# Grouping the transposed softmax probabilities by query tile in an attention block, with tile 3 taken first

## The chip, the cores and the metric

The kernel runs on one core of a Trainium2 chip. The metric is the device time of one execution in microseconds; the kernel before took 309.45 us (median of 3 runs, 309.11 to 309.55). Below, PE is the matmul engine, ACT the scalar engine, DVE the vector engine, POOL the GpSimd engine, SP the engine that issues the DMAs.

## The reference, cut to what matters

For two sequences of 512 rows of width 256: attention with 16 heads that share one key, which is also the value; then a residual sum and layer norm; then a feed-forward net on the half of the rows that a router picks; then another sum and layer norm. The change touches only the attention:

```
k = x @ W_lat + b_lat                      # 512 x 128, key and value of all heads
q = x @ W_d + b_d                          # per head 512 x 128
att = softmax(where(causal, q k^T / sqrt(128), -inf))
y = att @ k
out = concat(y) @ W_proj + b_proj
```

## The kernel before

**Units and periods.** A unit is one head of one sequence: 32 units. The code runs in periods, software-pipelined by hand: in period p the engines work on unit p (scores, softmax), unit p+1 (query projection), unit p-1 (transposing the probabilities, product with the values) and unit p-2 (output projection). Periods 3 to 12 are a hardware loop, the others are written out. Periods 18 to 27 also hold, in small pieces, the layer norm and the router of sequence 0: one "early piece" and one "late piece" a period on DVE (`early_piece` L944, `late_piece` L966). In periods 13 to 28 POOL also splits a part of the feed-forward weights.

**Precision.** Most products are made of three fp32r matmuls, hi*hi, hi*lo, lo*hi (`product`, L355). So each operand that comes out of PSUM is split: ACT copies the rounded high part, DVE subtracts it from the PSUM bank to get the low part.

**Tiles.** 512 queries are four tiles j of 128, 512 keys four tiles i. Because of the mask, query tile j has scores only for keys of tiles 0 to j. For each j, DVE adds the mask, takes the negated maximum and writes the scaled scores to SBUF (`maxima`, L885), ACT takes the exponential and the row sums (`exps`, L710), DVE takes the reciprocal of the sums (L936), and the tiles are scaled: tile 3 on ACT (L755), tiles 2, 1, 0 on DVE (L941), at the end of the period. In the next period PE transposes the ten 128x128 blocks P(j,i) in three turns (`turn`, L441), each turn into one PSUM bank, and ACT and DVE split what each turn has left in the bank (`turned`, L717 and L895).

**Before, a turn is a key tile.** Turn 0 is the four blocks of key tile 0, bank `ps_t0`; turn 1 the three of key tile 1, bank `ps_t1`; turn 2 the blocks (3,3), (2,2), (3,2), again in `ps_t0`. Block (3,3) is kept in plain fp32 (`pT_last`). Each key tile lies in one run of columns of `pT_hi` and `pT_lo`, and `values` (L493) makes one product for each key tile: 512, 384 and 256 columns wide, then the fp32 block.

**Order of one period.** PE: scores of tiles 3 and 2, turns 0 and 1, scores of 1 and 0, queries of the next unit (six matmuls of 512 columns), turn 2, output projection (twelve of 256), values. ACT: high part of y; turned 0 and 1; exponentials of 3 and 2; query high part; turned 2; exponentials of 1 and 0; scaling of tile 3. DVE: low part of y (`yT_lo`); maxima of 3; early piece; turned 0; maxima of 2; turned 1; maxima of 1 and 0; query low part; turned 2; reciprocal; late piece; scaling of 2, 1, 0. POOL: once all three scalings are done, it splits the next weights (four instructions, six in periods 13 to 28).

Turn 2 writes the bank that turn 0 used, so PE waits at L448 for DVE's turned 0. Turn 0 waits for all scalings (L446, L447). The last periods differ: period 31 makes no queries, and there turn 2 comes after the output projection, so the values follow turn 2 at once; period 32 is the same with gather matmuls in place of the scores.

Of the kernel before, what the change touches and what calls it, by code (L numbers as in the profile page):

```python
# [34 lines left out]
P = 128  # L35
# [17 lines left out]
PT_OFF = {2: 0, 1: 2 * P, 0: 5 * P}  # L53
PT_COLS = 9 * P


def mk_layer_kernel(nc, x, W_lat, b_lat, W_d, b_d, W_proj, b_proj, router_w, router_b,
                    w1, b1, w2, b2, out):
    with ExitStack() as top:
# [30 lines left out]
        negmax = sb("negmax", [P, 2, TILES])  # L90
        sums = sb("sums", [P, 2, TILES])
# [122 lines left out]
        def p_tile(s, j):  # L214
# [139 lines left out]
        def _(pe):  # L354
# [86 lines left out]
            def turn(at, n):  # L441

                p, s = at.p, at.place(-1)
                tiles, dst, _, _ = turns[n]
                if n == 0:
                    wait(pe, norm_act, p)  # L446
                    wait(pe, norm_dve, p * 3)  # L447
                wait(pe, pt_lo_done, p * 3 - (3, 4, 2)[n])  # L448
                if n == 1 and at.fixed - 1 in (AT_TURN, AT_SELECT, AT_RANK):

                    pe.wait_ge({AT_TURN: score_row_done, AT_SELECT: rank_row_done, AT_RANK: rank_done}[at.fixed - 1][0], 1)
                if at.fixed == 1 and n < CH:
                    pe.wait_ge(x_split, CH + n + 1)
                a = 0
                for i in tiles:
                    for j in range(i, TILES):
                        last = pe.transpose(dst[:, a:a + P], p_tile(s, j)[:, i * P:(i + 1) * P], ident[:, :])  # L457
                        a += P
                last.then_inc(pt_ready, 1)
# [33 lines left out]
            def values(at):  # L493

                p, b = at.p, at.batch(-1)
                if at.fixed - 1 == b * HEADS:
                    pe.wait_ge(k_split, b + 1)
                    pe.wait_ge(k_last_done, b + 1)
                wait(pe, y_lo_done, p - 1)
                for i in range(TILES - 1):  # L500
                    wait(pe, pt_lo_done, p * 3 - 2 + i)
                    n = (TILES - i) * P
                    t = slice(PT_OFF[i], PT_OFF[i] + n)
                    product(ps_y[:, SEQ - n:], (k_hi[b][:, i, :], k_lo[b][:, i, :]),
                            (pT_hi[:, t], pT_lo[:, t]), i == 0, False)
                wait(pe, pt_last_done, p)
                pe.matmul(ps_y[:, SEQ - P:], k_last[b][:, :], pT_last[:, :], start=False, stop=True).then_inc(y_ready, 1)  # L507
# [168 lines left out]
        def _(act):  # L676
# [40 lines left out]
            def turned(at, n):  # L717
                wait(act, pt_ready, at.p * 3 - 2 + n)
                if n == 2:
                    act.copy(pT_last[:, :], ps_t0[:, 0:P]).then_inc(pt_last_done, 1)  # L720
                act.copy(pT_hi[:, turns[n][3]], turns[n][2]).then_inc(pt_hi_done, 1)  # L721

            def period(at):
# [118 lines left out]
        def _(dve):  # L842
# [52 lines left out]
            def turned(at, n):  # L895
                wait(dve, pt_hi_done, at.p * 3 - 2 + n)
                _, _, src, dst = turns[n]
                dve.tensor_tensor(pT_lo[:, dst], src, pT_hi[:, dst].bitcast(F32), ALU.subtract).then_inc(pt_lo_done, 1)  # L898

            def period(at):  # L900
                p = at.p
                if at.live(0):
                    wait(dve, scores_ready, p * 3 + 1)
                if at.live(-2):
                    wait(dve, y_hi_done, p - 1)
                    dve.tensor_tensor(yT_lo[:, :], ps_y[:, :], yT_hi[:, :].bitcast(F32),  # L906
                                      ALU.subtract).then_inc(y_lo_done, 1)
                if at.live(0):
                    maxima(at, (3,))
                early_piece(at)  # L910
                if at.live(0):
                    wait(dve, scores_ready, p * 3 + 2)
                if at.live(-1):
                    turned(at, 0)
                if at.live(0):
                    maxima(at, (2,))
# [7 lines left out]
                if at.fixed == 0:  # L924
                    x_low(1, 1)
                    k_low(0)
                if at.live(1) and at.fixed >= 0:
# [3 lines left out]
                if at.live(-1):  # L931
                    turned(at, 2)
                s = at.place(0)
                if at.live(0):
                    wait(dve, exp_done, p * 4 + 4)
                    dve.reciprocal(rinv[:, s, :], sums[:, s, :]).then_inc(rinv_done, 1)  # L936
                late_piece(at)
                if at.live(0):
                    wait(dve, rinv_done, p + 1)
                    for j in (2, 1, 0):  # L940
                        dve.tensor_scalar(p_tile(s, j), p_tile(s, j), rinv[:, s, j:j + 1], None,  # L941
                                          ALU.mult).then_inc(norm_dve, 1)
# [350 lines left out]
```

## Time and profile before

| | |
|---|---|
| median of 3 runs | 309.45 us |
| the profiled execution's own time | 309.75 us |
| its span | 307.9 us |
| PE busy | 290.8 us (94%) |
| DVE busy | 229.6 us (75%) |
| ACT busy | 211.8 us (69%) |
| POOL busy | 147.0 us (48%) |
| matmul instructions | 1962 |

The span is the stretch in which instructions ran; the execution's own time is 1.85 us longer. Matmuls overlap in the pipeline, so a matmul's record is longer than the distance to the next one's start: the pace of PE is read from starts. Below, a period is measured from one start of the fp32 value matmul (L507) to the next.

### The profile page before, as it was taken

How to read it: one execution, taken by the hardware profiler on the slowest of the kernel's cores; microseconds unless marked ns; L12 is line 12 of the kernel's file. 1: busy time of each engine (PE TensorE's matmuls, PEld its weight loads, DVE VectorE, ACT ScalarE, POOL GpSimd, SP SyncE). 2: the span in 40 equal slices, each digit the busy share in tenths (PEclk: the TensorE clock that was granted, in tenths of full speed). 3: DMA queues.
4: the chain of work that ended last, by engine and by line, in shares of the span. 5: the costliest groups of instructions: out<-in, count | busy, mean ns of one | idle time of the engine just before them, and what ended most of it. 6: DMA issues, size and time to landing. Idle time of an engine off the chain costs nothing.

```text
span 307.9 us, 6338 instructions
## 1 busy us (share of the span) xinstructions
PE 290.8 (94%) x1962; PEld 262.5 (85%) x1962; DVE 229.6 (75%) x698; ACT 211.8 (69%) x585; POOL 147.0 (48%) x202
## 2 busy tenths in 40 slices
PE   7999999999999999999999998999999999985991
PEld 4878999999999999999998797788999999875990
DVE  2678777777777777778888878977887775886574
ACT  3688777777777777777776785686877777541632
POOL 3557433333333485555575564577583111672021
PEclk9999999999999999999999999999999999998998
DMA  6591111111111111111111111111100000000013
GB/s 192 103 326 48 35 36 34 34 34 34 34 34 34 34 35 36 34 38 34 34 36 34 35 36 35 35 26 44 27 19 27 21 0 0 3 0 2 0 35 104
DMA packets 17739, 13.44 MB, mean 44 GB/s; under 512 B 1433, under 2 KB 17458, under 8 KB 17714
## 3 DMA queue, kind: packets, MB, share of 16 engines
q1 hardware_dynamic: 17714, 13.13, 14.8%
q8 instruction: 13, 0.21, 0.3%
q14 instruction: 12, 0.10, 0.1%
HBM read 12.07 MB, written 1.05 MB: 43 GB/s over the span
## 4 chain that ended last, share of the span: by engine, by line
PE 78%; DVE 12%; ACT 4%; issue 2%; SPq 1%; DMA 1%; POOLq 0%; DVEq 0%; ACTq 0%
PE bank L358 15%; PE bank L360 14%; PE bank L359 14%; PE bank L457 10%; PE ps_out L358 5%; PE ps_out L359 5%; PE ps_out L360 5%; PE bank L507 2%; PE bank L437 2%; DVE ties L1055 1%; DVE sel L1034 1%; DVE probs L891 1%; DVE beats L1050 1%; DVE pT_lo L898 1%; PE bank L545 1%
## 5 line engine op out<-in xcount | busy, mean ns | idle before, releaser
L714 ACT ACTIVATE probs<-probs,negmax 128x512 f32<-128x512 f32 (+3 forms) x128 | 72.6, 575 | 13.1 <-DVE negmax L891 11.8
L1158 POOL TENSOR_TENSOR wd_hi<-wd_raw,zero 128x256 fp32r<-128x256 f32 x32 | 23.8, 743 | 95.0 <-DVE probs L941 89.0
L721 ACT CAST pT_hi<-bank 128x512 fp32r<-128x512 f32 (+2 forms) x96 | 43.5, 488 | 32.7 <-PE bank L457 32.7
L891 DVE CUSTOM_DVE_ANT_0 probs<-bank,mask_row 128x512 f32<-128x512 f32 (+3 forms) x128 | 59.1, 481 | 0.6 <-PE bank L360 0.6
L898 DVE TENSOR_TENSOR pT_lo<-bank,pT_hi 128x512 fp32r<-128x512 f32 (+2 forms) x96 | 52.8, 551 | 7.3 <-ACT pT_hi L721 7.2
L457 PE MATMUL bank<-ident,probs 128*128 128x128 f32 x320 | 45.7, 273 | 2.1 <-DVE pT_lo L898 2.1
L457 PEld LDWEIGHTS bank<-ident,probs 128*128 128x128 f32 x320 | 37.9, 140 | 9.7 <-DVE pT_lo L898 4.2
L358 PE MATMUL ps_out<-wp_hi,yT_hi 128*128 128x256 f32 x128 | 38.7, 302 | 0.1
L358 PE MATMUL bank<-kT_hi,qT_hi 128*128 128x512 f32 (+2 forms) x96 | 37.6, 392 | 0.2 <-DVE qT_lo L845 0.2
L906 DVE TENSOR_TENSOR yT_lo<-bank,yT_hi 128x512 fp32r<-128x512 f32 x32 | 22.1, 690 | 20.1 <-PE bank L360 14.0
L360 PE MATMUL ps_out<-wp_hi,yT_lo 128*128 128x256 f32 x128 | 36.1, 282 | 0.0
L359 PE MATMUL ps_out<-wp_lo,yT_hi 128*128 128x256 f32 x128 | 36.1, 282 | 0.0
L358 PE MATMUL bank<-pT_hi,k_hi 128*128 128x512 f32 (+2 forms) x96 | 32.9, 343 | 0.6 <-DVE pT_lo L898 0.6
L360 PE MATMUL bank<-kT_hi,qT_lo 128*128 128x512 f32 (+2 forms) x96 | 32.5, 339 | 0.0
L359 PE MATMUL bank<-pT_lo,k_hi 128*128 128x512 f32 (+2 forms) x96 | 32.4, 337 | 0.0
L359 PE MATMUL bank<-kT_lo,qT_hi 128*128 128x512 f32 (+2 forms) x96 | 32.3, 336 | 0.0
L845 DVE SCALAR_TENSOR_TENSOR qT_lo<-bank,bias_cols,qT_hi 128x384 fp32r<-128x384 f32 x32 | 19.8, 618 | 16.8 <-ACT qT_hi L684 16.8
L360 PE MATMUL bank<-pT_hi,k_lo 128*128 128x512 f32 (+2 forms) x96 | 32.2, 335 | 0.0
L1158 POOL TENSOR_TENSOR wp_hi<-wp_raw,zero 128x256 fp32r<-128x256 f32 x32 | 24.2, 757 | 15.8 <-DVE probs L941 15.8
L755 ACT ACTIVATE probs<-probs,rinv 128x512 f32<-128x512 f32 x32 | 23.2, 724 | 8.1 <-DVE rinv L936 8.1
L941 DVE TENSOR_SCALAR probs<-probs,rinv 128x384 f32<-128x384 f32 (+2 forms) x96 | 28.0, 348 | 0.8
L358 PE MATMUL bank<-xT_hi,wd_hi 128*128 128x512 f32 x64 | 27.8, 434 | 0.2 <-DVE negmax L891 0.2
(146 smaller groups left out, 763.2 us busy)
## 6 DMA issues: line engine op xcount, KB each, us to landing
wd_raw<-in_L_attn_W_d SPq DMA_DIRECT2D x32, 128.0 KB, 2.2
wp_raw<-in_L_attn_W_proj SPq DMA_DIRECT2D x32, 128.0 KB, 2.1
wf_raw<-in_L_ffn_w SPq DMA_DIRECT2D x2, 1024.0 KB, 7.3
x_nat<-in_L_attn_x SPq DMA_DIRECT2D x4, 256.0 KB, 3.1
out<-x SPq DMA_DIRECT2D x3, 256.0 KB, 3.1
out<-x SPq DMA_DIRECT2D x2, 128.0 KB, 1.9
wlat_raw<-in_L_attn_W_lat SPq DMA_DIRECT2D x1, 128.0 KB, 3.5
bproj_all<-in_L_attn_b_proj SPq DMA_DIRECT2D x1, 128.0 KB, 3.4
```

The source lines that it names most:

```text
L358: pe.matmul(dst, lh, rh, start=first, stop=False, skip_group_check=check)
L359: pe.matmul(dst, lh, rl, start=False, stop=False, skip_group_check=check)
L360: return pe.matmul(dst, ll, rh, start=False, stop=last, skip_group_check=check)
L457: last = pe.transpose(dst[:, a:a + P], p_tile(s, j)[:, i * P:(i + 1) * P], ident[:, :])
L714: act.activation(p_tile(s, j), p_tile(s, j), ACT.Exp, bias=negmax[:, s, j:j + 1], scale=-1.0, accum_out=sums[:, s, j:j + 1]).then_inc(exp_ ...
L721: act.copy(pT_hi[:, turns[n][3]], turns[n][2]).then_inc(pt_hi_done, 1)
L755: act.mul(p_tile(at.place(0), 3), p_tile(at.place(0), 3), rinv[:, at.place(0), 3:4]).then_inc(norm_act, 1)
L891: dve.tensor_tensor_reduce(p_tile(s, j), score_bank[j], mask_row[:, (TILES - 1 - j) * P:], -SCALE, -MASKED, ALU.add, ALU.min, accum_out=ne ...
L898: dve.tensor_tensor(pT_lo[:, dst], src, pT_hi[:, dst].bitcast(F32), ALU.subtract).then_inc(pt_lo_done, 1)
L906: dve.tensor_tensor(yT_lo[:, :], ps_y[:, :], yT_hi[:, :].bitcast(F32), ALU.subtract).then_inc(y_lo_done, 1)
L941: dve.tensor_scalar(p_tile(s, j), p_tile(s, j), rinv[:, s, j:j + 1], None, ALU.mult).then_inc(norm_dve, 1)
L1158: pool.tensor_tensor(hi, src, nothing, ALU.add).then_inc(hi_done, 1)
```

## The change

1. The turns are regrouped by query tile. Turn 0 is (3,0), (3,2), (3,1), (3,3) in `ps_t0`, turn 1 is (2,1), (2,0), (2,2) in `ps_t1`, turn 2 is (1,1), (0,0), (1,0) in `ps_t0`. Each has three blocks to split; `pT_last` now comes with turn 0. The blocks get places in `pT_hi` and `pT_lo` (now 11 blocks wide) such that each turn and each product reads or writes places at an even distance.
2. `turn` waits less at first: turn 0 for tile 3 scaled, turn 1 for tile 2 scaled, turn 2 for all.
3. `values` makes four products in place of three: key tile 2 for queries 2 and 3 (256 columns), the fp32 block, key tile 0 for queries 2 and 3 (256); then, after turn 2 is split, key tile 1 (384) and key tile 0 for queries 0 and 1 (256).
4. ACT takes the exponential of tile 3 before turned 0, and turned 2 before the query high part.
5. DVE begins a period with a memset of one column and the maxima of tile 3, then `yT_lo`, the maxima of 2, the early piece, turned 0, turned 1, the maxima of 1 and 0, turned 2, and then the query low part. At the end it scales tile 2 before the late piece, tiles 1 and 0 after it.

```diff
-PT_OFF = {2: 0, 1: 2 * P, 0: 5 * P}
-PT_COLS = 9 * P
+PT_SLOT = {0: range(2, 10, 2), 1: range(0, 15, 5), 2: range(7, 11, 2)}
+PT_COLS = 11 * P
...
-        turns = [([0], ps_t0, ps_t0[:, :], slice(PT_OFF[0], PT_OFF[0] + 4 * P)),
-                 ([1], ps_t1, ps_t1[:, 0:3 * P], slice(PT_OFF[1], PT_OFF[1] + 3 * P)),
-                 ([3, 2], ps_t0, ps_t0[:, P:3 * P], slice(PT_OFF[2], PT_OFF[2] + 2 * P))]
+        turns = [([(3, 0), (3, 2), (3, 1), (3, 3)], ps_t0, 8, 1),
+                 ([(2, 1), (2, 0), (2, 2)], ps_t1, 5, 1),
+                 ([(1, 1), (0, 0), (1, 0)], ps_t0, 0, 2)]
...
+        def turned_to(pT, n):
+            _, _, slot, step = turns[n]
+            return pT[:, :].rearrange("p (a c) -> p a c", c=P)[:, slot:slot + 2 * step + 1:step, :]
+        def values_of(pT, i, j0, j1):
+            slots = PT_SLOT[i][j0 - i:j1 - i]
+            return pT[:, :].rearrange("p (a c) -> p a c", c=P)[:, slots[0]:slots[-1] + 1:slots.step, :]
...
                 if n == 0:
                     wait(pe, norm_act, p)
+                    wait(pe, pt_last_done, p - 1)
+                elif n == 1:
+                    wait(pe, norm_dve, p * 3 - 2)
+                else:
                     wait(pe, norm_dve, p * 3)
+                    wait(pe, pt_last_done, p)
                 wait(pe, pt_lo_done, p * 3 - (3, 4, 2)[n])
...
-                for i in range(TILES - 1):
-                    wait(pe, pt_lo_done, p * 3 - 2 + i)
-                    n = (TILES - i) * P
-                    t = slice(PT_OFF[i], PT_OFF[i] + n)
-                    product(ps_y[:, SEQ - n:], (k_hi[b][:, i, :], k_lo[b][:, i, :]),
-                            (pT_hi[:, t], pT_lo[:, t]), i == 0, False)
+                wait(pe, pt_lo_done, p * 3 - 1)
+                keys(2, 2, 4, first=True)
                 wait(pe, pt_last_done, p)
-                pe.matmul(ps_y[:, SEQ - P:], k_last[b][:, :], pT_last[:, :], start=False, stop=True).then_inc(y_ready, 1)
+                pe.matmul(ps_y[:, SEQ - P:], k_last[b][:, :], pT_last[:, :], start=False, stop=False,
+                          skip_group_check=True)
+                keys(0, 2, 4)
+                wait(pe, pt_lo_done, p * 3)
+                keys(1, 1, 4)
+                keys(0, 0, 2, last=True).then_inc(y_ready, 1)
...
             def period(at):          # ACT
+                if at.live(0):
+                    exps(at, (3,))
                 if at.live(-1):
                     wait(act, y_ready, p - 1)
                     turned(at, 0)
...
                 if at.live(0):
-                    exps(at, (3, 2))
+                    exps(at, (2,))
+                if at.live(-1):
+                    turned(at, 2)
                 if at.live(1) and at.fixed >= 0:
                     split_queries(p + 1, at.place(1), at.head(1))
-                if at.live(-1):
-                    turned(at, 2)
...
             def period(at):          # DVE
+                if at.live(0):
+                    dve.memset(begun[:, :], 0.0)
+                    maxima(at, (3,))
+                    wait(dve, scores_ready, p * 3 + 2)
                 if at.live(-2):
                     wait(dve, y_hi_done, p - 1)
                     dve.tensor_tensor(yT_lo[:, :], ps_y[:, :], yT_hi[:, :].bitcast(F32),
                                       ALU.subtract).then_inc(y_lo_done, 1)
                 if at.live(0):
-                    maxima(at, (3,))
+                    maxima(at, (2,))
                 early_piece(at)
...
                 if at.live(0):
                     wait(dve, exp_done, p * 4 + 4)
                     dve.reciprocal(rinv[:, s, :], sums[:, s, :]).then_inc(rinv_done, 1)
+                    wait(dve, rinv_done, p + 1)
+                    normalise(at, (2,))
                 late_piece(at)
                 if at.live(0):
-                    wait(dve, rinv_done, p + 1)
-                    for j in (2, 1, 0):
+                    normalise(at, (1, 0))
```

## Rows read from the trace of the kernel before

**Rows 1.** The page, part 1: busy time, share and instructions of each engine.
```profile
PE 290.8 (94%) x1962; PEld 262.5 (85%) x1962; DVE 229.6 (75%) x698; ACT 211.8 (69%) x585; POOL 147.0 (48%) x202
```

**Rows 2.** Periods 17, 20 to 27 as windows: length, busy of engines, clock, DMA, GB/s.
```profile
136.73:144.24 7.51, 7.51 (x53) 6.91 (x52) 5.52 (x18) 5.73 (x17) 4.34 (x6) 1.00 0.11 35
...
159.25:167.18 7.93, 7.74 (x53) 6.78 (x51) 7.02 (x23) 5.39 (x16) 5.71 (x8) 1.00 0.11 33
167.18:175.45 8.27, 7.85 (x53) 6.73 (x52) 7.43 (x25) 5.62 (x16) 4.57 (x6) 1.00 0.12 33
175.45:183.13 7.68, 7.68 (x52) 6.84 (x51) 6.81 (x25) 6.10 (x17) 4.34 (x6) 1.00 0.13 36
183.13:192.37 9.24, 8.18 (x57) 7.24 (x56) 7.25 (x20) 5.84 (x18) 4.33 (x6) 1.00 0.11 29
192.37:200.78 8.41, 7.94 (x53) 6.73 (x52) 7.57 (x25) 5.62 (x16) 4.57 (x6) 1.00 0.12 33
200.78:208.88 8.10, 7.87 (x53) 6.92 (x52) 6.68 (x23) 7.06 (x19) 5.58 (x7) 1.00 0.12 33
208.88:217.19 8.31, 8.31 (x72) 7.36 (x71) 5.90 (x18) 5.49 (x17) 5.64 (x7) 1.00 0.12 35
217.19:225.14 7.95, 7.95 (x56) 7.35 (x55) 6.83 (x22) 6.60 (x18) 6.33 (x7) 1.00 0.12 34
```

**Rows 3.** The waits of the whole span: total us, times, longest.
```profile
PEld bank L457 <- DVE pT_lo L898: 4.2, 5, 1.5
```

**Rows 4.** Timeline of period 16: start, duration, engine, line, operation, idle before.
```profile
130.34 0.69 DVE L906 TENSOR_TENSOR yT_lo<-bank,yT_hi 128x512 fp32r<-128x512 f32 x1 [0.73 <-PE bank L360]
...
130.95 0.68 DVE L891 CUSTOM_DVE_ANT_0 probs<-bank,mask_row 128x512 f32<-128x512 f32 x1
...
132.05 0.69 DVE L898 TENSOR_TENSOR pT_lo<-bank,pT_hi 128x512 fp32r<-128x512 f32 x1 [0.42 <-ACT pT_hi L721]
...
132.22 0.74 ACT L714 ACTIVATE probs<-probs,negmax 128x512 f32<-128x512 f32 x1
...
132.84 0.20 ACT L714 ACTIVATION_READ_ACCUMULATOR probs<-probs,negmax 128x1 f32 x1
...
133.65 0.36 PE L358 MATMUL ps_out<-wp_hi,yT_hi 128*128 128x256 f32 x1
...
134.58 0.26 ACT L720 COPY pT_last<-bank 128x128 f32<-128x128 f32 x1
...
134.72 0.39 ACT L721 CAST pT_hi<-bank 128x256 fp32r<-128x256 f32 x1
...
135.16 0.40 PE L358 MATMUL bank<-pT_hi,k_hi 128*128 128x512 f32 x1
...
136.24 0.88 DVE L941 TENSOR_SCALAR probs<-probs,rinv 128x384 f32<-128x384 f32 x3
...
136.73 0.39 PE L507 MATMUL bank<-pT_last,k_last 128*128 128x128 f32 x2
```

**Rows 5.** Groups by line and shape, 100 to 200 us: busy us, mean ns.
```profile
L898 DVE TENSOR_TENSOR pT_lo<-bank,pT_hi 128x384 fp32r<-128x384 f32 x13 | 7.2, 550 | 0.0
...
L721 ACT CAST pT_hi<-bank 128x384 fp32r<-128x384 f32 x13 | 6.3, 486 | 0.0
```

**Rows 6.** Timelines of DVE, POOL and PE in periods 20, 25 and 31.
```profile
161.58 1.54 DVE L1025 TENSOR_SCALAR x<-x,mv,rstd 128x256 f32<-128x256 f32 x2
...
162.18 0.80 POOL L1158 TENSOR_TENSOR wp_hi<-wp_raw,zero 128x256 fp32r<-128x256 f32 x1
...
163.78 0.55 PE L457 MATMUL bank<-ident,probs 128*128 128x128 f32 x3 [0.19 <-DVE pT_lo L898]
...
164.08 0.36 PE L358 MATMUL ps_out<-wp_hi,yT_hi 128*128 128x256 f32 x1
...
204.08 0.47 PE L358 MATMUL bank<-xT_hi,wd_hi 128*128 128x512 f32 x1 [0.23 <-DVE negmax L891]
...
253.47 0.39 PE L358 MATMUL bank<-pT_hi,k_hi 128*128 128x256 f32 x1
```

More of the change, by code:

```diff
@@ L90, in mk_layer_kernel @@
         negmax = sb("negmax", [P, 2, TILES])
+        begun = sb("begun", [P, 1])
         sums = sb("sums", [P, 2, TILES])
@@ L217, in mk_layer_kernel, with turned_from @@
         score_bank = {3: ps_s3[:, :], 2: ps_s2[:, 0:3 * P], 1: ps_s10[:, 2 * P:4 * P], 0: ps_s10[:, 0:P]}
-        turns = [([0], ps_t0, ps_t0[:, :], slice(PT_OFF[0], PT_OFF[0] + 4 * P)),
-                 ([1], ps_t1, ps_t1[:, 0:3 * P], slice(PT_OFF[1], PT_OFF[1] + 3 * P)),
-                 ([3, 2], ps_t0, ps_t0[:, P:3 * P], slice(PT_OFF[2], PT_OFF[2] + 2 * P))]
+        turns = [([(3, 0), (3, 2), (3, 1), (3, 3)], ps_t0, 8, 1),
+                 ([(2, 1), (2, 0), (2, 2)], ps_t1, 5, 1),
+                 ([(1, 1), (0, 0), (1, 0)], ps_t0, 0, 2)]
+        for tiles, _, slot, step in turns:
+            for a, (j, i) in enumerate(tiles):
+                assert j == 3 and i == 3 or PT_SLOT[i][j - i] == slot + a * step
+        def turned_from(n):
+            return turns[n][1][:, 0:3 * P].rearrange("p (a c) -> p a c", c=P)
+        def turned_to(pT, n):
[4 more added lines that the diff above has]
+            return pT[:, :].rearrange("p (a c) -> p a c", c=P)[:, slots[0]:slots[-1] + 1:slots.step, :]
         class Period:
@@ L453, in turn @@
                     pe.wait_ge(x_split, CH + n + 1)
[L454 to L458, printed above, removed]
+                for a, (j, i) in enumerate(tiles):
+                    last = pe.transpose(dst[:, a * P:(a + 1) * P], p_tile(s, j)[:, i * P:(i + 1) * P], ident[:, :])
                 last.then_inc(pt_ready, 1)
@@ L499, in values, with keys @@
                 wait(pe, y_lo_done, p - 1)
-                for i in range(TILES - 1):
-                    wait(pe, pt_lo_done, p * 3 - 2 + i)
-                    n = (TILES - i) * P
-                    t = slice(PT_OFF[i], PT_OFF[i] + n)
-                    product(ps_y[:, SEQ - n:], (k_hi[b][:, i, :], k_lo[b][:, i, :]),
-                            (pT_hi[:, t], pT_lo[:, t]), i == 0, False)
-                wait(pe, pt_last_done, p)
-                pe.matmul(ps_y[:, SEQ - P:], k_last[b][:, :], pT_last[:, :], start=False, stop=True).then_inc(y_ready, 1)
+                def keys(i, j0, j1, first=False, last=False):
+                    return product(ps_y[:, j0 * P:j1 * P], (k_hi[b][:, i, :], k_lo[b][:, i, :]),
+                                   (values_of(pT_hi, i, j0, j1), values_of(pT_lo, i, j0, j1)), first, last, True)
+                wait(pe, pt_lo_done, p * 3 - 1)
+                keys(2, 2, 4, first=True)
+                wait(pe, pt_last_done, p)
+                pe.matmul(ps_y[:, SEQ - P:], k_last[b][:, :], pT_last[:, :], start=False, stop=False,
[4 more added lines that the diff above has]
+                keys(0, 0, 2, last=True).then_inc(y_ready, 1)
             def turn_scores(b, dst):
@@ L718, in turned @@
                 wait(act, pt_ready, at.p * 3 - 2 + n)
-                if n == 2:
-                    act.copy(pT_last[:, :], ps_t0[:, 0:P]).then_inc(pt_last_done, 1)
-                act.copy(pT_hi[:, turns[n][3]], turns[n][2]).then_inc(pt_hi_done, 1)
+                if n == 0:
+                    act.copy(pT_last[:, :], ps_t0[:, 3 * P:]).then_inc(pt_last_done, 1)
+                act.copy(turned_to(pT_hi, n), turned_from(n)).then_inc(pt_hi_done, 1)
             def period(at):
@@ L915, in period @@
                 if at.live(0):
-                    maxima(at, (2,))
                     wait(dve, scores_ready, p * 3 + 3)
@@ L926, in period @@
                     k_low(0)
+                if at.live(-1):
+                    turned(at, 2)
                 if at.live(1) and at.fixed >= 0:
@@ L936, in period, with normalise @@
                     dve.reciprocal(rinv[:, s, :], sums[:, s, :]).then_inc(rinv_done, 1)
+                    wait(dve, rinv_done, p + 1)
+                    normalise(at, (2,))
                 late_piece(at)
                 if at.live(0):
-                    wait(dve, rinv_done, p + 1)
-                    for j in (2, 1, 0):
-                        dve.tensor_scalar(p_tile(s, j), p_tile(s, j), rinv[:, s, j:j + 1], None,
-                                          ALU.mult).then_inc(norm_dve, 1)
+                    normalise(at, (1, 0))
+            def normalise(at, js):
+                s = at.place(0)
+                for j in js:
+                    dve.tensor_scalar(p_tile(s, j), p_tile(s, j), rinv[:, s, j:j + 1], None,
+                                      ALU.mult).then_inc(norm_dve, 1)
             def early_piece(at):
```

8 lines of the change are left out of this document (2 added, 6 removed).

## The prediction

> **What bounds the kernel now.** I read part 1 of the page first: PE is busy 94% of the span [rows 1]. Then the windows of whole periods: an undisturbed period takes 7.51 us with PE busy in all of it and the clock at 1.00, its upper level of 2.4 GHz [rows 2]. So about twenty of the 32 periods are PE's alone, and what ACT and DVE do there costs nothing while it comes in time. The list of waits shows where it doesn't: PE's transpositions wait five times for DVE's low part, 4.2 us in all [rows 3]. The windows place them: periods 20 to 27 take 7.93, 8.27, 7.68, 9.24, 8.41, 8.10, 8.31 and 7.95 us, 5.8 us above eight times 7.51 [rows 2]. Some 1.5 us of that are matmuls of the router in windows 23, 26 and 27; the rest, about 4.3 us, is what the change can win there. The timeline of a quiet period then gives the slack of each step [rows 4].
>
> **The deadline at turn 2.** I count from the fp32 value matmul, 129.22 us in period 16 (136.73 less one period) [rows 4]. DVE begins at +1.12 (130.34). Turn 2 may start when DVE's turned 0 has ended, because of the bank. PE reaches the output projection behind it at 133.65 [rows 4]. After a wait the three transpositions take 0.30 (163.78 to 164.08) [rows 6], and from DVE's end to their start I estimate 0.05, so turned 0 must end by 133.65 - 0.35 = 133.30, at +4.08.
> Before: yT_lo to the next start 0.61 (130.34 to 130.95), the same for the maxima, then turned 0 of 512 columns, 0.69 [rows 4]. With an early piece E the chain is 1.91 + E, ending at +3.03 + E: E above 1.05 stalls PE. Without one it waits for ACT and ends at 132.74, 0.56 early.
> After: memset m, maxima 0.61, yT_lo 0.61, maxima of tile 2 0.48 (384 columns take 0.13 less than 512: 0.55 against 0.69 for the low parts), E, turned 0 of 384 columns 0.55 [rows 5]: 2.25 + m + E. The trace has no one-column memset. From above it is a whole small instruction, 0.20 (ACT's one-column read, 132.84), from below nothing, as it might overlap; I take 0.08, the pace of small instructions in line. So the chain ends at +3.45 + E, and E above 0.63 stalls PE: 0.42 less slack.
> Without a piece ACT decides: maxima of 3 end at +1.12 + 0.08 + 0.69; then 0.03 to the exponential, 0.62 and 0.10 for it and its read (132.22 to 132.84 and on), 0.15 for pT_last (134.58 to 134.72), 0.49 for the high part [rows 4, 5], 0.05 over to DVE, 0.55. That ends at +3.88: 0.20 before the deadline, against 0.56 before. Quiet periods stay at 7.51, but with little left.
>
> **Values in quiet periods.** Twelve matmuls where there were nine, the same 3456 columns. The nine take 136.73 - 135.16 = 1.57, 0.454 ns a column; the twelve of the projection take 135.16 - 133.65 = 1.51, of which some 0.08 is the first one's start [rows 4], so 0.119 for 256 columns against 0.116 at that pace. That is 0.003 for each of three more, 0.01 a period, 0.3 us over all; bounds 0 and 0.8 us. Reading blocks at even distances I cost at nothing (each is a run of 128 columns). Turn 2's split ends at about +5.9 and the last two products need it at about +7.0, so that wait is hidden; so is the query low part, some 0.5 later than before, which the next scores need over 1 us afterwards.
>
> **Periods 20 to 27.** The piece's own length matters. In period 20 two scalings of 256 columns take 1.54 us in DVE [rows 6], while the three of the softmax, 768 columns in all, take 0.88 [rows 4]; the slow ones run while POOL works, and their ends follow the ends of POOL's instructions, which take 0.74 to 0.80 (the one from 162.18 ends at 162.98, the two scalings at 163.12) [rows 6]. So a piece that starts later ends at one of POOL's next boundaries. I replayed each period: start, plus 1.78 (0.08 + 0.61 + 0.61 + 0.48), then each instruction of the piece to POOL's next boundary, then 0.55, against +4.08 (later by the router's matmuls). Against the before this gives: 20: +0.4; 21: +0.3; 22: -0.2; 23: -0.1; 24: +0.5; 25: -0.55; 26: +0.4 (a boundary is caught or just missed, 0 or 0.75); 27: +0.2 (likewise). Two gains are firm. In 21, 22 and 24 DVE started late, 0.2 to 0.4, because of the chain turned 0, maxima 2, queries, exponentials, late piece, scaling; it is shorter now. In 25 the queries waited for the maxima of 3 behind yT_lo (they start at 204.08, after a wait; at the normal distance it would be 203.5) [rows 6]; now the maxima come first and 0.55 goes. Sum +0.95, between -1.5 (pieces at their bare length) and +2.5 (each boundary missed).
>
> The Trainium skill ("SBUF — State Buffer", Who interferes with whom) says that a DVE instruction in a two-port mode, or with two SBUF inputs against a reading GpSimd instruction, blocks for a whole instruction of the other. By that rule a piece never slips between; with free overlap the pieces would be short and the change would win, the second rival below. The 1.54 for two small scalings [rows 6] speaks for the rule.
>
> **The ends of the pipeline.** In periods 31 and 32 the values follow turn 2 directly. Before, 1.23 us of products (512 and 384 columns) lay ahead of the one that needs turn 2, and 0.57 behind; PE came to it at 253.47, only 0.05 late [rows 6]. After, 0.92 lies ahead (256, fp32, 256) and 0.88 behind (384, 256): 0.31 more after the wait. ACT's part is 0.49 in place of 0.15 + 0.39, DVE's 0.55 in place of 0.41, and the first matmul after a wait costs some 0.05 more: +0.4 in each, +0.85 in both, bounds +0.5 and +1.1. Nothing gives it back: what follows waits for y. In period 1, where PE waits the same way, the two products ahead of the wait are shorter but turn 2 is split 0.65 us earlier on DVE, so PE leaves 0.3 earlier; in period 2 DVE, late by a piece of period 1 and with the longer chain, takes it back: +0.1.
>
> **Sum.** 0.3 + 0.95 + 0.85 + 0.1 = +2.2 us on the profiled execution: 309.75 + 2.2 = 311.95. That execution stands 0.3 above the median, so on the scale of the median 311.6 us.
>
> **Rivals.**
> The first is that quiet periods stall as well. If the 0.20 of slack is gone (a slower memset, slower waits in the loop), every period is late by the excess. Before, the loop's ACT and DVE had 0.4 us of idle there [rows 4], so nothing shows how exact my 0.20 is. It decides from 0.20 on; with 0.10 more the price is 0.1 x 25 = 2.5 us on top of the forecast, 314.1. Against it: each piece of the sum is a measured distance.
> The second ends on the other side: the pieces are short where they now stand. If they ran at some 0.35 an instruction, the deadline would be met within 0.3 us in periods 20, 21, 24 and 26, and of about 4.3 us of stalls some 1.0 would be left. That is -3.3, with 0.3, 0.85 and 0.1 against it -2.05; I take half, since POOL would still hold some of them: -1.0, so 308.4. It decides once two instructions of a piece take under 0.9 us together. Against it: POOL starts its six instructions when the scalings end, and they last beyond the piece in every period.
> The third: the moved steps balance. If the boundaries in 24, 26 and 27 are caught, 1.1 goes, and if the drain costs 0.5 instead of 0.85, 0.35 more: +0.5 or so, 309.9, which is within what can be told from no change (0.2%, 0.6 us).
>
> **How the numbers follow.** Forecast 0.52, first rival 0.13, second 0.15, third 0.20. Faster by over 0.2% (below 308.8): the second, 0.14. Within 0.2% (to 310.1): most of the third and the edge of the forecast, 0.20. Slower: 0.66. The forecast's own range is 310.4 to 312.9. The whole: from 309.0, since below lies little but the second rival, to 313.2, which leaves out most of the first: about 0.2 outside.
>
> **What would show it.** Right: quiet periods at 7.51 or 7.52; windows 20, 21, 24 longer than before, 22, 25 shorter, waits of the transpositions for DVE's low part above 4.2 us; in periods 31 and 32 a wait of some 0.4 ahead of a 384-column product. Wrong: quiet periods over 7.6 (first rival); pieces of two instructions under 0.9 us (second); a drain as long as before.

## The result, and the profile after

The changed kernel takes 312.29 us, median of four runs (311.74 to 313.66), against 309.31 (309.11 to 309.55): a ratio of 1.0094, 95% interval 1.0064 to 1.0125. It is slower by 3.0 us; 2.2 were predicted. The median lies in the predicted range of 309.0 to 313.2; its profiled execution is the longest of its four, 313.66 us with a span of 312.0, against 309.75 and 307.9 before.

Part 1 of its page and the row of the granted clock answer to [rows 1]: PE has 96 matmuls more (three in each of 32 units) and the same share, and the clock falls near the end.

```profile
PE 293.3 (94%) x2058; PEld 269.8 (86%) x2058; DVE 233.7 (75%) x730; ACT 211.8 (68%) x585; POOL 146.9 (47%) x202
...
PEclk9999999999999999999999999999999999996897
```

A new counting serves both kernels from here on: a period lasts from the first scores matmul of 512 columns to the next such one, as the old end of a period (the last value product) has itself moved. The windows of the changed kernel are a quiet period, periods 20 to 27, 31 and 32, and the rest (length, busy of the five engines, clock, DMA share, GB/s):

```profile
122.75:130.28 7.53, 7.53 (x55) 7.07 (x54) 5.58 (x19) 5.74 (x16) 4.36 (x6) 1.00 0.13 36
...
160.42:168.63 8.21, 7.73 (x56) 7.00 (x54) 7.47 (x26) 5.74 (x16) 5.70 (x8) 1.00 0.12 34
168.63:177.17 8.54, 7.73 (x56) 7.00 (x54) 7.77 (x27) 5.74 (x16) 4.58 (x6) 1.00 0.10 32
177.17:185.07 7.90, 7.90 (x60) 7.44 (x58) 6.84 (x25) 5.90 (x17) 4.48 (x7) 1.00 0.11 33
185.07:193.89 8.82, 7.84 (x57) 7.10 (x54) 7.16 (x21) 6.17 (x18) 4.19 (x6) 1.00 0.12 33
193.89:203.04 9.15, 7.72 (x55) 6.99 (x54) 8.48 (x25) 5.75 (x17) 4.32 (x6) 1.00 0.11 29
203.04:211.09 8.05, 8.05 (x76) 7.54 (x74) 6.37 (x22) 6.67 (x19) 5.69 (x7) 1.00 0.12 35
211.09:219.45 8.36, 8.18 (x63) 7.44 (x60) 6.71 (x21) 5.82 (x18) 5.65 (x7) 1.00 0.12 34
219.45:227.42 7.97, 7.83 (x56) 7.08 (x55) 6.63 (x21) 6.07 (x17) 6.36 (x7) 1.00 0.11 34
...
250.00:256.63 6.63, 6.40 (x50) 6.05 (x49) 4.74 (x17) 4.80 (x14) 1.48 (x2) 1.00 0.00 0
256.63:263.38 6.75, 6.53 (x55) 6.32 (x53) 3.30 (x8) 4.23 (x10) 1.47 (x2) 1.00 0.01 2
263.38:312.00 48.62, 36.56 (x286) 34.93 (x284) 32.60 (x96) 19.07 (x53) 15.26 (x17) 0.88 0.07 22
```

From these windows and the like ones of before, the 4.1 us between the two spans come apart so:

| stretch | before | after | difference | predicted |
|---|---|---|---|---|
| to the first scores | 11.50 | 11.86 | +0.36 | - |
| periods 0 to 2 | 20.28 | 20.57 | +0.29 | +0.1 |
| 3 to 19 | 127.61 | 127.99 | +0.38 | part of 0.3 |
| 20 | 7.93 | 8.21 | +0.28 | +0.4 |
| 21 | 8.27 | 8.54 | +0.27 | +0.3 |
| 22 | 8.12 | 7.90 | -0.22 | -0.2 |
| 23 | 8.79 | 8.82 | +0.03 | -0.1 |
| 24 | 8.42 | 9.15 | +0.73 | +0.5 |
| 25 | 8.68 | 8.05 | -0.63 | -0.55 |
| 26 | 8.17 | 8.36 | +0.19 | +0.4 |
| 27 | 7.51 | 7.97 | +0.46 | +0.2 |
| 28 to 30 | 22.53 | 22.58 | +0.05 | part of 0.3 |
| 31 and 32 | 12.63 | 13.38 | +0.75 | +0.85 |
| the rest | 47.46 | 48.62 | +1.16 | - |

The start (input transfers) and the rest are not of the change: over all profiles of this study the first scores come between 11.29 and 12.00 us, and the rest is a matter of the clock. In both kernels PE stands still while DVE works on `ties`, as the timelines of PE show, of after and of before (the bracket is the idle time ahead of the matmuls):

```profile
283.46 0.24 PE L543 MATMUL bank<-ones_bf,beats 128*128 128x1 bf16 x4 [3.44 <-DVE ties L1085]
```

```profile
280.59 0.24 PE L521 MATMUL bank<-ones_bf,beats 128*128 128x1 bf16 x4 [3.39 <-DVE ties L1055]
```

Then the granted clock falls to 0.50, the lower level of 1.2 GHz. Windows of PE near the end of that stretch (length, busy, clock, DMA, GB/s), of after and of before:

```profile
289.00:290.00 1.00, 1.00 (x7) 0.50 0.09 16
290.00:291.00 1.00, 1.00 (x8) 0.79 0.00 0
```

```profile
284.00:285.00 1.00, 1.00 (x7) 0.50 0.00 0
285.00:286.00 1.00, 1.00 (x9) 0.84 0.00 0
```

By such windows of 1 us the low stretch lasted from about 283.6 to 290.4 after (6.8 us; 0.79 in the window from 290 is 0.42 us at 0.50 and the rest at 1.00), and from 281.9 to 285.3 before (3.4 us). Without the start and the rest the profiled pair differs by 2.6 us.

Last, the timeline of a quiet period of the changed kernel, the one whose scores start at 130.28, to be laid beside [rows 4]: maxima of tile 3 first, the memset of one column, the low parts of turned 0 and 1 in one group, and the three transpositions of turn 2.

```profile
131.17 0.69 DVE L915 CUSTOM_DVE_ANT_0 probs<-bank,mask_row 128x512 f32<-128x512 f32 x1 [0.74 <-issue]
131.19 0.06 DVE L929 MEMSET begun<- 128x1 f32 x1
...
133.28 1.02 DVE L921 TENSOR_TENSOR pT_lo<-bank,pT_hi 128x384 fp32r<-128x384 f32 x2 [0.34 <-ACT pT_hi L743]
...
134.21 0.49 PE L475 MATMUL bank<-ident,probs 128*128 128x128 f32 x3
```

Turned 0 (the first of the two low parts, 0.55) ends at 133.83, and the transpositions start at 134.21 with no wait. Of the 0.38 between, PE would need some 0.06 to start behind DVE's end, as it did in period 20 of before (163.73 to 163.78), so 0.32 are to spare. The record of the memset lies beneath that of the maxima (131.17 to 131.86), and the next instruction of DVE starts 0.61 after the maxima do (131.78), as in [rows 4]: no time of its own is seen for it.

### The profile page after: what moved, and what is told of

The parts are those of the page before. It is cut to its first block, busy times and chain, and to the rows that moved or that the text cites. A ratio compares the mean times of both kernels' runs of the same rounds, so it can differ in the third digit from the quotient of the medians.

```text
span 312.0 us, 6577 instructions
## 1 busy us (share of the span) xinstructions
PE 293.3 (94%) x2058; PEld 269.8 (86%) x2058; DVE 233.7 (75%) x730; ACT 211.8 (68%) x585; POOL 146.9 (47%) x202
## 4 chain that ended last, share of the span: by engine, by line
PE 69%; DVE 16%; ACT 7%; issue 5%; SPq 1%; DMA 1%; POOLq 0%; DVEq 0%; ACTq 0%
PE bank L373 13%; PE bank L375 13%; PE bank L374 13%; PE bank L475 10%; PE ps_out L373 5%; PE ps_out L374 5%; PE ps_out L375 4%; ACT probs L736 2%; DVE probs L971 2%; PE bank L452 2%; PE bank L524 2%; DVE pT_lo L921 2%; DVE ties L1085 1%; DVE sel L1064 1%; ACT qT_hi L706 1%
## 5 line engine op out<-in xcount | busy, mean ns | idle before, releaser
L921 DVE TENSOR_TENSOR pT_lo<-bank,pT_hi 128x384 fp32r<-128x384 f32 x96 | 50.4, 552 | 19.1 <-ACT pT_hi L743 19.1
L743 ACT CAST pT_hi<-bank 128x384 fp32r<-128x384 f32 x96 | 42.9, 483 | 20.6 <-PE bank L475 20.6
L373 PE MATMUL bank<-pT_hi,k_hi 128*128 128x256 f32 (+1 forms) x128 | 41.2, 322 | 0.5 <-DVE pT_lo L921 0.5
L375 PE MATMUL bank<-pT_hi,k_lo 128*128 128x256 f32 (+1 forms) x128 | 38.3, 299 | 0.0
L374 PE MATMUL bank<-pT_lo,k_hi 128*128 128x256 f32 (+1 forms) x128 | 37.9, 296 | 0.0
L373 PE MATMUL bank<-kT_hi,qT_hi 128*128 128x512 f32 (+2 forms) x96 | 35.1, 366 | 0.2 <-DVE qT_lo L869 0.2
L971 DVE TENSOR_SCALAR probs<-probs,rinv 128x384 f32<-128x384 f32 (+2 forms) x96 | 29.0, 349 | 1.1
L736 ACT ACTIVATION_READ_ACCUMULATOR probs<-probs,negmax 128x1 f32 x128 | 25.6, 200 | 0.0
L373 PEld LDWEIGHTS bank<-pT_hi,k_hi 128*128 128x128 f32 x128 | 24.4, 190 | 1.3 <-DVE pT_lo L921 1.1
```

Source lines behind the costliest of these rows:

```text
L373: pe.matmul(dst, lh, rh, start=first, stop=False, skip_group_check=check)
L374: pe.matmul(dst, lh, rl, start=False, stop=False, skip_group_check=check)
L375: return pe.matmul(dst, ll, rh, start=False, stop=last, skip_group_check=check)
L736: act.activation(p_tile(s, j), p_tile(s, j), ACT.Exp, bias=negmax[:, s, j:j + 1], scale=-1.0, accum_out=sums[:, s, j:j + 1]).then_inc(exp_ ...
L743: act.copy(turned_to(pT_hi, n), turned_from(n)).then_inc(pt_hi_done, 1)
L921: dve.tensor_tensor(turned_to(pT_lo, n), turned_from(n), turned_to(pT_hi, n).bitcast(F32), ALU.subtract).then_inc(pt_lo_done, 1)
```

## The experiments

The change is called the change; "before" and "after" are the two kernels. Each kernel ran on the chip beside runs of before, and its ratio is to those.

**Three more matmuls alone.** Before, with the 512-column value product cut in two of 256 (the flags of the other value products, which only switch off a check of the groups, are left out here):

```diff
+                    if i == 0:
+                        for h in range(2):
+                            u = slice(PT_OFF[0] + 2 * h * P, PT_OFF[0] + 2 * (h + 1) * P)
+                            product(ps_y[:, 2 * h * P:2 * (h + 1) * P], (k_hi[b][:, 0, :], k_lo[b][:, 0, :]),
+                                    (pT_hi[:, u], pT_lo[:, u]), h == 0, False, True)
+                        continue
```

> The kernel before, with its 512-column value product cut into two of 256 columns (blocks still side by side), so three more matmuls a unit and no other change. Quiet periods went from 7.505 to 7.525 us with the change. Theory: the three more matmuls are all of it, 0.02 us a period: quiet periods at 7.52 to 7.53, the whole +0.5 us. Rival: the reading at even distances, or the waits that DVE and ACT are now nearer to, cost it; then quiet periods stay at 7.51 here and the whole at +0.1 or less.

Measured: 310.4 us, before 309.81 in the same runs: ratio 1.002 (1.0005 to 1.0034). Its quiet period is 7.53, periods 3 to 19 take 128.07 for 127.61, both as expected. Cut at the first value matmul, period 10 shows where that arises. PE's windows of this kernel, and then of the later one "The early piece on before", which keeps nine matmuls (length, busy, clock, DMA, GB/s); in before the two parts are 5.79 and 1.71, in after 5.69 and 1.84:

```profile
84.48:90.27 5.79, 5.79 (x42) 1.00 0.15 45
90.27:92.01 1.74, 1.74 (x16) 1.00 0.00 0
```

```profile
84.89:90.71 5.82, 5.82 (x43) 1.00 0.15 45
90.71:92.42 1.71, 1.71 (x14) 1.00 0.00 0
```

In this kernel the values alone grow: 1.739 against 1.712 as the mean of periods 3 to 17, so 0.027 for three matmuls. In the changed kernel 0.13 is added in the values and 0.11 leaves the first part; about 0.08 of both is one start after small matmuls that moved (the first scores matmul takes 0.31 to the next before, 0.23 after), which leaves +0.02 on balance. Two independent readings thus give 0.02 to 0.03 with the three matmuls, and reading the blocks at even distances isn't needed for it. The other kernel warns how far this goes: with nine matmuls, and in periods 3 to 17 the same instructions in the same order as before, it too has 7.53, all of it ahead of the values (5.82 against 5.79). What makes this other 0.02 was not found.

**Maxima of tile 2 behind turned 0.** After, with this moved alone:

```diff
                 if at.live(0):
-                    maxima(at, (2,))
                 early_piece(at)
                 if at.live(-1):
                     turned(at, 0)
                 if at.live(0):
+                    maxima(at, (2,))
                     wait(dve, scores_ready, p * 3 + 3)
```

> The changed kernel with one move undone: DVE does the maxima of tile 2 after turned 0 again, not before it (and so behind the early piece too). Theory: in the router's periods turned 0 is the last thing PE waits for, so the 0.48 us of the maxima come off each period that waits there, as far as POOL's boundaries let it: periods 20, 21, 23, 24 and 26 together shorter by 1 to 2 us, the whole by 1 to 2 us, quiet periods unchanged. Rival 1: the pieces end at POOL's boundaries wherever they start, so nothing or up to a boundary (0.75) here and there comes off: -0.5 to +0.5. Rival 2: the loss is in the clock of the last 30 us; then this moves nothing beyond noise.

Measured: 309.52 us, ratio 0.9988 (0.9973 to 1.0003). Periods 20 to 27 take 63.89 in place of 67.00, above all 23 (7.90 for 8.82), 24 (8.36 for 9.15) and 20 (7.69 for 8.21). That is 3.1 us, more than the 1 to 2 expected. The chain of the prediction, shorter by 0.48, thus decides these periods, and more strongly than its own length, because the pieces in it end at other instructions of POOL. In period 23 the three instructions of the piece take 0.38, 0.41 and 0.83 here, and 0.32, 0.91 and 0.82 in after: the second one now starts just ahead of POOL's, and it is POOL's that grows, from 0.74:

```profile
186.97 0.41 DVE L1083 TENSOR_SCALAR beats<-score_row,score 128x384 bf16<-128x384 f32 x1
...
187.04 0.93 POOL L1190 TENSOR_TENSOR wp_lo<-wp_raw,wp_hi 128x256 fp32r<-128x256 f32 x1
```

The 63.89 is also 2.0 less than the 65.89 of before. So in the router's periods the rest of the change is a gain, and this one move turned it into a loss. Elsewhere this kernel still pays (periods 0 to 2 +0.7, 3 to 19 +0.3, 31 and 32 +0.9 against before), so the whole can't be told from before.

**The early piece behind turned 0.** After, with only this:

```diff
-                early_piece(at)
                 if at.live(-1):
                     turned(at, 0)
+                early_piece(at)
```

> The changed kernel with the early piece of DVE put behind turned 0 instead of ahead of it. Theory: the piece leaves the chain to turn 2; periods 20, 21, 23, 24 and 26 (8.21, 8.54, 8.82, 9.15, 8.36 us) lose their stall at turn 2, but DVE has 7.0 to 7.6 us of work in them, so they end near 7.6 to 8.0 and the sum of 20 to 27 is 2 to 3 us shorter. Rival: DVE is so full there that what leaves turn 2 comes back as a wait of the next scores for the query low part or of turn 1 for its scaling; then less than 1 us.

Measured: 307.93 us, ratio 0.9928 (0.9907 to 0.995), 4.4 below after. Periods 20 to 27 take 62.40 in place of 67.00, 4.6 less where 2 to 3 were expected; period 18 grows by 0.12, to 7.65. Periods 20 and 23 by PE's windows:

```profile
160.25:167.77 7.52, 7.52 (x55) 1.00 0.12 35
...
183.40:191.03 7.63, 7.63 (x56) 1.00 0.14 38
```

Period 20 is quiet again: its whole excess was the piece ahead of turned 0.

**Less of POOL's work beside the pieces.** After, with the feed-forward weights split in eight parts of 512 columns, mostly ahead of period 20:

```diff
-        WF_PERIODS = range(13, 29)
+        WF_PERIODS = [13, 14, 15, 16, 17, 18, 28, 29]
```

> The changed kernel with POOL's split of the feed-forward weights taken out of periods 19 to 27: eight parts of 512 columns in periods 13 to 18, 28 and 29 instead of sixteen of 256 in 13 to 28. Theory: DVE's pieces end when POOL's running instruction ends. In period 23 the last two instructions of the piece wait for the two weight splits that are gone: 0.8 to 1.3 us shorter. In period 24 the last wait goes: 0.4 shorter. In 20, 21 and 26 the pieces wait for POOL's wd and wp splits, which stay: no change beyond 0.2. The whole -1.2 to -1.8. Rival: the pieces are slow by themselves or by what ACT and PE do; then no period changes.

Measured: 311.2 us, ratio 1.0038 (1.0022 to 1.0054). Period 23 takes 7.84 (after 8.82) and 24 takes 8.64 (9.15), and 20 to 27 together are 1.5 shorter, all as expected; 20 and 21, where POOL still splits the other weights, keep 8.21 and 8.54. The DVE piece of period 23 with POOL at work, in the changed kernel, POOL's two instructions beneath it:

```profile
187.74 0.32 DVE L1080 TENSOR_SCALAR beats<-score_row,score 128x128 bf16<-128x128 f32 x1
187.99 0.91 DVE L1083 TENSOR_SCALAR beats<-score_row,score 128x384 bf16<-128x384 f32 x1
188.82 0.82 DVE L1085 SCALAR_TENSOR_TENSOR ties<-score_row,score,earlier 128x128 bf16<-128x128 f32 x1
...
187.94 0.74 POOL L1188 TENSOR_TENSOR wf_hi<-wf_raw,zero 128x256 fp32r<-128x256 f32 x1
...
188.76 0.73 POOL L1190 TENSOR_TENSOR wf_lo<-wf_raw,wf_hi 128x256 fp32r<-128x256 f32 x1
```

and in this kernel, where POOL's last instruction ended at 187.69:

```profile
187.44 0.33 DVE L1080 TENSOR_SCALAR beats<-score_row,score 128x128 bf16<-128x128 f32 x1
187.69 0.41 DVE L1083 TENSOR_SCALAR beats<-score_row,score 128x384 bf16<-128x384 f32 x1
188.02 0.34 DVE L1085 SCALAR_TENSOR_TENSOR ties<-score_row,score,earlier 128x128 bf16<-128x128 f32 x1
```

The same three instructions end 1.90 us after the first one's start with POOL and 0.92 without, 0.98 less, and the period is 0.98 shorter. 188.90 and 189.64, the ends of the slow two, lie 0.15 to 0.22 behind the ends of POOL's, 188.68 and 189.49. The Trainium skill ("SBUF — State Buffer", Who interferes with whom) describes this as an exclusive lock on the port pair that DVE shares with GpSimd; the trace agrees, with 0.91 against 0.41 and 0.82 against 0.34.

**Turn 2 ahead of the projection in the last period.** After, with

```diff
                 else:
+                    if at.fixed == UNITS:
+                        turn(at, 2)
                     project(at)
-                    if at.live(-1):
+                    if at.live(-1) and at.fixed != UNITS:
                         turn(at, 2)
```

> The changed kernel with turn 2 of period 32 put ahead of the output projection, as in all earlier periods; period 31 stays. Theory: period 32 is longer than before by 0.39 us (6.75 against 6.36) because too little lies between turn 2 and the product that needs it; with 1.4 us of projection between, the wait goes and period 32 comes to 6.3 to 6.4, the whole -0.4. Rival: period 32 is bound by ACT's and DVE's chain of the gathered rows, and the wait only moves to turn 2; then 6.6 or more.

Measured: 312.77 us, ratio 1.01 (1.0073 to 1.0128). Period 32 stays, 6.76 for 6.75. The wait has only moved, to the first transposition:

```profile
259.29 0.52 PE L475 MATMUL bank<-ident,probs 128*128 128x128 f32 x3 [0.20 <-DVE pT_lo L923]
```

The 384-column product behind it, at 262.03, waits for nothing now: the values take 1.93 us in place of 2.39.

The rival came. The wait behind turn 2 did go, but turn 2 itself came too early for the bank that it writes, and from the start of the matmul before it to its own there are 0.48 us where 0.12 is usual. As one wait took the place of another of the same size, the experiment doesn't price the first; what the ends owe their 0.39 to is read from the rows of the change alone (below).

**The clock kept up in the rest.** Both kernels, with 16 idle matmuls (bf16, 512 columns) while DVE works on `ties`:

```diff
+            pe.wait_ge(gelu_done[0], FCH)
+            keep_awake(AWAKE_RANK)
             rank_cols(1, ps_t0)
```

> The kernel before, with 16 idle matmuls (bf16, 512 columns, on zeros, into a free bank) where PE waits 3.4 us for the router's comparison of sequence 1; the arithmetic of the outputs is the same. In the profile of the changed kernel the granted clock was 0.50 from about 283.6 to 290.2, in that of before from 281.9 to 285.3, each after this wait. Theory: the clock falls because PE had stood still; kept busy it stays at 1.00, and the part after the last scores is 58.5 to 59.5 us instead of 60.1 (or 61.4 where the clock stays low longer). Rival: the low clock comes from something else and stays; then 60 to 62.

> The changed kernel with the same 16 idle matmuls. Theory: of the 1.9 us by which its last part (from the scores of the last unit) is longer than before, 62.00 against 60.09, only the 0.75 of periods 31 and 32 is the change's and the rest is how long the clock stays low, which differs from run to run: with both kernels kept awake the last parts differ by 0.7 to 0.8. Rival: the change makes the end slower in another way; then they differ by 1.5 or more.

Measured: on before 307.73 us, ratio 0.9942 (0.9922 to 0.9962); on after 310.63, ratio 1.0041 (1.0024 to 1.0057). PE's windows on before and on after where the clock had been 0.50:

```profile
280.00:285.00 5.00, 4.75 (x55) 1.00 0.01 3
```

```profile
285.00:290.00 5.00, 5.00 (x45) 1.00 0.02 3
```

From the start of period 31 to the end it is 58.50 and 59.28, in place of 60.09 and 62.00. The remaining 0.78 is that of periods 31 and 32 (0.75 above), so behind them the change costs nothing. The five kernels of this study with the idle matmuls, two with the change and three without, all take 45.84 to 45.94 us behind period 32. This pair is the cleanest measure of the change: 2.9 us between the medians.

**The early piece on before.** Early piece behind turned 0 and the maxima of tile 2:

```diff
-                early_piece(at)
...
                 if at.live(-1):
                     turned(at, 0)
                 if at.live(0):
                     maxima(at, (2,))
+                early_piece(at)
+                if at.live(0):
                     wait(dve, scores_ready, p * 3 + 3)
```

> The kernel before, with its early piece put behind turned 0 and the maxima of tile 2. The same move in the changed kernel took 4.6 us off periods 20 to 27 (67.0 to 62.4). Theory: the place of the piece is what counts, not the regrouping: 20 to 27 go from 65.9 to 63 or 64 (the late pieces still hold up turn 0 here, and period 25 keeps its 8.7), and the whole to about 307.5 to 308, as good as the changed kernel with the move (307.9) or better, since the drain is not longer and there are no extra matmuls. Rival: the regrouping is needed for the gain, because all scalings stand behind the late piece; then 65 or more.

Measured: 306.88 us, ratio 0.9913 (0.9888 to 0.9937); periods 20 to 27 take 62.75 in place of 65.89, more of a gain than expected. The place of the piece brings its gain without any of the change. It isn't free: period 18 takes 7.83 here in place of 7.51.

**The maxima of tile 3 first, alone.** Before, with

```diff
+                if at.live(0):
+                    dve.memset(begun[:, :], 0.0)
+                    maxima(at, (3,))
                 if at.live(-2):
                     wait(dve, y_hi_done, p - 1)
                     dve.tensor_tensor(yT_lo[:, :], ps_y[:, :], yT_hi[:, :].bitcast(F32),
                                       ALU.subtract).then_inc(y_lo_done, 1)
-                if at.live(0):
-                    maxima(at, (3,))
```

> The kernel before with one part of the change alone: DVE begins the period with the memset and the maxima of tile 3, and the low part of y comes after them. Theory: this part is a gain. In period 25, where y's high part is late behind ScalarE's extra copy, the queries no longer wait for the maxima: 8.68 becomes 8.0 to 8.2; quiet periods 7.51 as before; the memset may add up to 0.1 to the stalls of 20, 21, 23, 24 and 26. The whole -0.2 to -0.6. Rival: the wait of period 25 only moves to turn 0's split, and nothing is gained.

Measured: 309.91 us, ratio 1.0002 (0.9983 to 1.0021): nothing over all, in an interval of 0.6 us to either side. Periods 25 and 26 by PE's windows, 8.68 and 8.17 before:

```profile
201.44:209.67 8.23, 8.23 (x74) 1.00 0.10 32
209.67:218.04 8.37, 8.17 (x60) 1.00 0.12 34
```

Period 25 gains 0.45 and 26 gives 0.20 back; 20 to 27 take 65.67 for 65.89, a gain of 0.2 that the medians can't show.

**What the experiments point to.** `b_best1` is before with the early piece moved, the eight periods for the feed-forward weights, and the 16 idle matmuls. `b_best2` adds the maxima of tile 3 first; `a_best` is after with the early piece, the eight periods and the idle matmuls.

> The kernel before with the three things that the runs point to: the early piece behind turned 0 and the maxima of 2, POOL's weight split out of periods 19 to 27, and the 16 idle matmuls. Theory: the gains add where they act in different places: -2.5 from the piece, -1.7 or more from the clock, -0.2 to -0.5 from POOL (most of its gain is already in the piece's move): 304.6 to 305.3. Rival: the weights split late (periods 28 and 29, two long instructions each) hold up what POOL does there; then 305.5 or more.

> The same as the last with the maxima of tile 3 first in the period as well (the memset with them). Theory: 0.3 to 0.6 less, from period 25: 304.2 to 304.9. Rival: without the early piece in the way the memset and the later low part of y cost as much as period 25 gains; then no difference.

> The changed kernel with the same three things as b_best1. Theory: what the change itself costs when the router's pieces are out of its way is the head 0.3, the quiet periods 0.5, the drain 0.8, and what it gains is the late pieces and period 25, some 0.5 to 1.0: 0.5 to 1.2 us slower than b_best1. Rival: with the pieces out of the way the regrouping pays; then it is as fast as b_best1 or faster.

Measured: 304.62 us, ratio 0.9833 (0.9808 to 0.9859); 304.56, ratio 0.9833 (0.9807 to 0.9859); 306.03, ratio 0.9882 (0.9859 to 0.9906). In the first one, which falls in the expected range, four of the router's periods are quiet (20, 21, 23 and 24), 22, 25 and 26 (7.94, 8.15 and 7.95) are longer mainly by the router's matmuls, and 27 has a new stall:

```profile
160.16:167.67 7.51, 7.51 (x53) 1.00 0.12 35
167.67:175.18 7.51, 7.51 (x54) 1.00 0.13 38
...
190.63:198.14 7.51, 7.51 (x54) 1.00 0.13 35
...
214.24:222.22 7.98, 7.78 (x53) 1.00 0.11 33
```

With most stalls of the pieces and of the clock gone on both sides, the change still costs 1.4 us by the medians, somewhat more than the 0.5 to 1.2 expected. In the profiled pair it is 0.29 in periods 0 to 2, 0.18 in 20 to 27 and 0.73 in 31 and 32. The maxima of tile 3 first make no difference there, as the rival said.

## Why the prediction was right, step by step

**Quiet periods** held in their mechanism: turned 0 is in time, so the first rival is out, though at 7.53 they lie 0.01 beyond the 7.51 or 7.52 that were to show it. The slack was taken too small, 0.20 for a measured 0.32, and the 0.08 for the memset too large: its record of 0.06 lies beneath the maxima. The term itself was under-sized: 0.02 a period for the three matmuls and not 0.01, in all 0.43 (0.38 + 0.05) instead of 0.3, and the warning given above, of a like 0.02 from elsewhere, applies to it.

**Periods 20 to 27** came as worked out: +1.11 for +0.95, with seven of eight signs right, 23 being even. The two gains called firm are there. The first, DVE's late start in 21, 22 and 24, shows alone in 22 (-0.22); in 21 and 24 PE had reached the queries 0.10 and 0.26 later than in a quiet period and no longer does, but the longer stall at turn 2 more than takes it back. The second is period 25 (-0.63), and moving the maxima of tile 3 alone gives 0.45 of it. The chain was the cause: taking the 0.48 of the maxima of tile 2 out of it took 3.1 us away, and taking the piece out 4.6. The second rival (short pieces) fell, with 0.91 and 0.82 for what takes 0.41 and 0.34 when POOL is still.

One number depends on the execution: period 23 of before took 8.79 here, and 8.23 in the kernel with idle matmuls, whose only edit lies 80 us later. The two traces show what differs. DVE's first comparison and POOL's instruction, of before and then of that kernel:

```profile
185.90 0.85 DVE L1050 TENSOR_SCALAR beats<-score_row,score 128x128 bf16<-128x128 f32 x1
...
185.93 0.73 POOL L1160 TENSOR_TENSOR wp_lo<-wp_raw,wp_hi 128x256 fp32r<-128x256 f32 x1
```

```profile
185.98 0.28 DVE L1052 TENSOR_SCALAR beats<-score_row,score 128x128 bf16<-128x128 f32 x1
...
186.03 0.82 POOL L1162 TENSOR_TENSOR wp_lo<-wp_raw,wp_hi 128x256 fp32r<-128x256 f32 x1
```

With 0.03 us between the two starts DVE's took 0.85, with 0.05 it took 0.28; the other two comparisons are long in both. The change then costs 1.1 to 1.7 us in these periods. That the sum came within 0.2 is partly luck: the replay gives the boundaries of one profiled execution, and a few hundredths of a microsecond move a period by 0.57.

The sign in the list of waits, that the transpositions' wait for DVE's low part rises, came too, but it has to be read on one engine in both lists. [rows 3] is the row of the weight load. PE's own row (total, times, longest), of before and then of after with the weight load's above it:

```profile
PE bank L457 <- DVE pT_lo L898: 2.1, 4, 1.1
```

```profile
PEld bank L475 <- issue: 7.9, 10, 1.8
...
PE bank L475 <- DVE pT_lo L921: 4.2, 6, 1.4
```

PE's own wait doubles, from 2.1 to 4.2. The weight load's idle time stands wholly under "issue" in after, 7.9, with no releaser; in before it was 4.2 under DVE and 1.3 under "issue". So the two figures of 4.2 are not the same thing, and the row that the prediction named can't be followed into the new trace.

**The ends.** Periods 31 and 32 take +0.36 and +0.39 for +0.4 each. The predicted wait ahead of a 384-column product is there in both, DVE's low part directly before it in the first:

```profile
255.02 0.56 DVE L921 TENSOR_TENSOR pT_lo<-bank,pT_hi 128x384 fp32r<-128x384 f32 x1 [0.45 <-ACT pT_hi L743]
...
255.12 0.28 PE L375 MATMUL bank<-pT_hi,k_lo 128*128 128x256 f32 x1
255.63 0.45 PE L373 MATMUL bank<-pT_hi,k_hi 128*128 128x384 f32 x1 [0.23 <-DVE pT_lo L921]
...
262.39 0.45 PE L373 MATMUL bank<-pT_hi,k_hi 128*128 128x384 f32 x1 [0.22 <-DVE pT_lo L921]
```

The brackets say 0.23 and 0.22, but they count from the modelled end of the matmul before. By starts, which is how PE's pace is read here, 255.12 to 255.63 is 0.51 where the usual distance is 0.12, so the wait costs 0.39, and in period 32 0.38: the 0.4 of the prediction. The values as a whole take 1.94 and 1.93 us before and 2.40 and 2.39 after; 0.10 and 0.07 come back ahead of them. In the kernels with the change the two periods take 6.61 to 6.63 (6.76 in one) and 6.75 or 6.76, and 6.26 or 6.27 and 6.36 or 6.37 in those without. That the costs are these is read from the rows; the one experiment on it exchanged the wait for another. In periods 0 to 2 the predicted shape came (period 1 -0.24, period 2 +0.51), but the giving back was larger than the gain: +0.3 for +0.1.

**The whole.** 2.6 us in the profiled pair without the start and the rest, 2.9 in the pair with the clock kept up, 3.0 by the first medians, against 2.2. Too small were the terms for the matmuls (0.3 for 0.43), for periods 0 to 2 (0.1 for 0.29) and for 20 to 27 (0.95 for 1.11, or 1.67 with the short period 23 of before); that of the ends was 0.1 too large. No cost of the change was found outside the terms. The low clock in the rest, which lengthened the profiled execution by another 1.2, is in both kernels and was in no term; with the start it puts that execution, at 313.66, above the predicted range. One sum of the prediction is wrong without bearing on the forecast: the third rival's 2.2 less 1.1 and 0.35 is +0.75, not +0.5, so it would have come to 310.2, just outside the 0.2% that it was to fall in.

## What to carry to other kernels

Where PE is full, ask of a moved step how long the chain to the next wait becomes, and what optional work (here a piece of the router) stands inside it: moving that piece behind the wait's releaser gave more than regrouping the work around it, on either kernel. A change of several moves is worth taking apart: here one of them, the maxima of tile 2 ahead of the wait's releaser, cost 3.1 us and hid a gain of 2.0 of the others. A DVE piece that runs beside GpSimd is to be costed by GpSimd's instructions, not by its own length. When an engine's idle stretch lets the clock fall late in a kernel, idle matmuls in it are worth a try before finer edits: here they gave 1.7 us on either kernel.

## What the runs showed of the hardware

The low clock after an idle stretch of the same length did not last equally long: 3.4 us at 0.50 in one profile and 6.8 in the other, after 3.4 us of standing still in both. The quiet period of nine value matmuls takes 7.51 in most kernels and 7.53 in one with the same instructions there; in `b_best1` it is 7.53 up to period 13 and 7.51 from 15 on. The same DVE piece can cost a period 0.57 more or less between two kernels that don't differ up to it, by whether one of its instructions takes 0.28 or 0.85 beside GpSimd. In period 23 of the changed kernel DVE's instruction of 0.91 started 0.05 us behind POOL's; with the maxima of tile 2 behind turned 0 it started 0.07 ahead and took 0.41, while POOL's took 0.93. But in before DVE's started 0.03 ahead of POOL's and took 0.85 all the same, so at such distances the recorded starts don't tell which engine is held up.
